# Attention, layer norm and FP4 feed-forward on one core: maxima transposed in 32 by 32 blocks on VectorE and split on GpSimd, loads of stacks and weights in other chunks, another order in the first chunk

## What is computed

```
q, k, v = (x w.T) * s + b          # 16 heads of 16, each weight 256x256
attn    = softmax(q k.T / sqrt(16))
x1      = layernorm(x + (attn v) w_o.T * s_o + b_o)
fq(t)   = blockwise FP4 quantise and dequantise, blocks of 16
h       = silu(fq(x1) fq(w_gate).T) * (fq(x1) fq(w_up).T)      # 704 wide
out     = layernorm(x1 + fq(h) fq(w_down).T)
```

## Time and profile before

| | |
|---|---|
| median of 3 runs | 2092.97 us (2092.76 to 2098.21) |
| profiled execution | 2092.96 us, span 2091.1 us |
| granted TensorE clock, mean | 0.993 |
| PE busy | 2026.4 us, 97% of the span |
| PEld busy | 1055.3 us, 50% |
| DVE busy | 1898.9 us, 91% |
| ACT busy | 1669.0 us, 80% |
| POOL busy | 799.2 us, 38% |
| chain that ended last | PE 83%, DVE 10%, ACT 4%, DMA 1% |
| stages, from the span's start | project to about 210 us, attend to about 1500 us, feed to 2091 us |

### The profile page before, as it was taken

How to read it: one execution, slowest core, us unless ns; L and a number is a source line. 1 busy time by engine, 2 the same in 40 slices (tenths; PEclk the granted TensorE clock), 3 DMA queues, 4 the chain that set the end, 5 groups by cost and what they waited for, 6 DMA issues and landing times.

```text
span 2091.1 us, 42075 instructions
## 1 busy us (share of the span) xinstructions
PE 2026.4 (97%) x15836; PEld 1055.3 (50%) x15836; DVE 1898.9 (91%) x2497; ACT 1669.0 (80%) x3246; POOL 799.2 (38%) x712
## 2 busy tenths in 40 slices
PE   8899999999999999999999999999889999999998
PEld 7677333333333333333333333333477777777776
DVE  4687999999999999999999999998299999999996
ACT  6566888888888888888888888888767777777775
POOL 3000599999100000000000000000168888888885
PEclk9999999999999999999999999999999999999999
DMA  7965632342243234224223322420212222222110
GB/s 211 270 226 214 113 55 49 54 68 48 43 70 57 43 58 64 48 44 76 51 43 63 59 48 48 74 48 13 89 42 61 59 61 61 61 61 61 61 31 21
DMA packets 106615, 153.09 MB, mean 73 GB/s; under 512 B 22124, under 2 KB 68972, under 8 KB 106412
## 3 DMA queue, kind: packets, MB, share of 16 engines
q1 hardware_dynamic: 98732, 142.79, 31.0%
q10 hardware_dynamic: 7392, 7.34, 1.1%
q0 software_dynamic: 288, 0.27, 0.1%
HBM read 89.53 MB, written 59.24 MB: 71 GB/s over the span
## 4 chain that ended last, share of the span: by engine, by line
PE 83%; DVE 10%; ACT 4%; DMA 1%; issue 1%; POOL 1%; SPq 0%; POOLq 0%; ACTq 0%; DVEq 0%
PE ps L860 25%; PE ps L915 23%; PE ps L1184 12%; DVE negmax L1024 9%; PE ps L1206 8%; PE ps L480 4%; PE ps L490 3%; PE ps L1173 3%; PE ps L1195 2%; ACT craw L983 2%; PE ps L1214 1%; DMA qk_parts<-parts 1%; PE ps L884 1%; ACT room L975 1%; PE ps L467 1%
## 5 line engine op out<-in xcount | busy, mean ns | idle before, releaser
L1024 DVE TENSOR_REDUCE negmax<-ps 128x1 f32<-128x1024 f32 x984 | 1189.1, 1221 | 28.6 <-PE ps L860 22.9
L975 ACT ACTIVATE room<-ps 128x512 f32<-128x512 f32 x2048 | 1102.6, 609 | 139.5 <-PE ps L884 109.9
L884 PE MATMUL ps<-qs,ks 50*128 50x512 f32 x2048 | 744.8, 448 | 0.7 <-ACT room L975 0.5
L860 PE MATMUL ps<-ks,qs 48*128 48x512 f32 x1968 | 717.6, 444 | 16.3 <-DVE negmax L1024 16.3
L915 PE MATMUL ps<-room,vals 128*17 128x256 f32 x8192 | 638.0, 385 | 11.3 <-ACT craw L983 1.5
L860 PEld LDWEIGHTS ps<-ks,qs 48*128 48x128 f32 x1968 | 289.8, 184 | 425.3 <-DVE negmax L1024 317.6
L1429 POOL TENSOR_TENSOR ctxT<-cin 128x256 f32<-128x256 f32 x64 | 58.6, 916 | 957.6 <-DMA cin<-rden 957.6
L915 PEld LDWEIGHTS ps<-room,vals 128*17 128x17 f32 x8192 | 139.3, 95 | 375.2 <-issue 206.7
L884 PEld LDWEIGHTS ps<-qs,ks 50*128 50x128 f32 x2048 | 303.7, 184 | 16.9 <-ACT room L975 12.4
L1184 PE MATMUL ps<-wguT,xqT 128*128 128x512 f32 (+1 forms) x1152 | 265.1, 384 | 2.1 <-DVE xqT L1357 2.1
L1184 PEld LDWEIGHTS ps<-wguT,xqT 128*128 128x128 f32 x1152 | 209.3, 189 | 58.6 <-issue 20.2
(11 more groups left out here) (109 smaller groups left out, 2171.4 us busy)
## 6 DMA issues: line engine op xcount, KB each, us to landing
qk_parts<-parts SPq DMA_DIRECT2D x64, 512.0 KB, 3.5
qs<-qk_parts SPq DMA_DIRECT2D x192, 128.0 KB, 4.6
ks<-qk_parts SPq DMA_DIRECT2D x192, 128.0 KB, 7.4
ctx_raw<-craw SPq DMA_DIRECT2D x64, 256.0 KB
cin<-ctx_raw SPq DMA_DIRECT2D x64, 128.0 KB
cin<-rden SPq DMA_DIRECT2D x64, 128.0 KB
xin<-in_L_attn_x_dram SPq DMA_DIRECT2D x32, 256.0 KB, 4.7
out_dram<-fin SPq DMA_DIRECT2D x64, 128.0 KB, 1.7
```

The lines of the kernel that those rows point to most:

```text
L860: return nc.tensor.matmul(ps[:, MX + 2 * (item[i.k, u] % 2) + bank, :], qs[rows, i.slot(RING), pair, t * P:(t + 1) * P], ks[rows, i.slot(R ...
L884: nc.tensor.matmul(ps[:, score_bank(i, s * GH + n), :], ks[rows, slot, pair, kt * P:(kt + 1) * P], qs[rows, slot, pair, qh * BANK:(qh + 1) ...
L975: nc.scalar.activation(prob[:, prob_slot(i, s), score_order(i)[n], :], ps[:, score_bank(i, s * GH + n), :], ACT.Exp, scale=float(D) ** -0. ...
L1024: nc.vector.tensor_reduce(negmax[:, j.slot(RING), max_column(u):max_column(u) + 1], ps[:, bank:bank + 2, :], AX.XY, ALU.max, negate=True). ...
```

## The change

The transpose of the maxima leaves TensorE. VectorE turns `negmax` in blocks of 32 by 32 (`turn`, into `turned_rows`, 128x32), GpSimd makes the high part and the remainder (`part`), and SyncE moves them with eight DMAs of 4 KB each, in pieces of 128 bytes. The turn takes no place in the alternation of the banks (`items` has units alone).

`AHEAD` goes from 4 to 6: the maxima of the next group are done and turned at step 10 instead of 12, and twelve units of group 1 instead of eight run in `project`, four in each of chunks 12 to 14.

GpSimd calls `part` once before the weight quantisation (group 1), once after every eight operations of it, and for the remaining groups after it. It waits each time until that group's maxima are turned.

In `project` the query stack of group 0 is loaded in chunk 2 and the key stack in chunk 3 (both in chunk 2 before), those of group 1 in chunks 8 and 9 (both in 5 before). The first two weights for the scales are loaded in chunks 5 and 7 instead of 0 and 2, so that VectorE makes those scales at the end of chunks 6 and 8. The FFN weights are loaded behind the stack of group 2 instead of ahead of it. Within a block of queries and keys the product with the remainder of x is last. In the first chunk the transposes of w_k and w_v stand before query block 0, with their copies.

```diff
-AHEAD = 4
+AHEAD = 6
 LEAD = 2 * AHEAD
-ARRIVED = 64
+BQ = 32
+ARRIVED = 16 * 2 * (P // BQ)
 PRODUCTS = ((0, 0), (0, 1), (1, 0))
+PROJECTED = ((0, 0), (1, 0), (0, 1))
...
-    def transpose(self, nc, bank, negmax, ident, i):
-        nc.tensor.transpose(bank[0:MU, 0:P], negmax[:, i.slot(RING)], ident[:, :]).then_inc(self.psum, 1)
-
-    def split(self, nc, dve, bank, i, done):
-        dve.wait_ge(self.psum, i.lin(1, 1))
-        wait(dve, self.arrived, i.lin(ARRIVED))
-        nc.vector.tensor_copy(self.mrow[:, 0], bank[0:MU, 0:P]).then_inc(self.chain, 1)
-        dve.wait_ge(self.chain, i.lin(1, 1))
-        nc.vector.tensor_tensor(self.mrow[:, 1], bank[0:MU, 0:P], self.mrow[:, 0].bitcast(F32),
-                                ALU.subtract).then_inc(done, 1)
...
+    def turn(self, nc, dve, negmax, i):
+        wait(dve, self.parted, i.lin(2))
+        nc.vector.transpose(self.turned_rows[:, :], negmax[:, i.slot(RING)]).then_inc(self.turned, 1)
+
+    def part(self, nc, pool, i):
+        pool.wait_ge(self.turned, i.lin(1, 1))
+        wait(pool, self.arrived, i.lin(ARRIVED))
+        nc.gpsimd.tensor_copy(self.mrow[:, 0], self.turned_rows[:, :]).then_inc(self.parted, 1)
+        pool.wait_ge(self.parted, i.lin(2, 1))
+        nc.gpsimd.tensor_tensor(self.mrow[:, 1], self.turned_rows[:, :], self.mrow[:, 0].bitcast(F32),
+                                ALU.subtract).then_inc(self.parted, 1)
+
+    def into_stack(self, sp, qs, i):
+        sp.wait_ge(self.parted, i.lin(2, 2))
+        for part in range(2):
+            rows = qs[KR + part:P:HALF, i.slot(RING)].bitcast(F32).rearrange("a j (t b q) -> a (j t) b q", b=P // BQ,
+                                                                             q=BQ)
+            for b in range(P // BQ):
+                sp.dma_start(rows[:, :, b, :], self.mrow[b * BQ:(b + 1) * BQ, part].bitcast(F32)
+                             ).then_inc(self.arrived, 16)
...
-        if i.k < TURN:
-            return list(range(first, first + MAX_PER))
-
-        return [u if MU <= u < MU + LEAD else None for u in range(first - 1, first - 1 + MAX_PER)]
+        return [u if u < MU + LEAD else None for u in range(first, first + MAX_PER)]
...
-        return {0: 0, 2: 1, NCH - 3: 2}.get(i.k)
+        return {MAX_FROM + 1: 0, MAX_FROM + 3: 1, NCH - 3: 2}.get(i.k)
...
-            group = {MAX_FROM - 2: 0, MAX_FROM + 1: 1}.get(i.k)
-            if group is not None:
-                sp.wait_ge(ones_ready, 2)
-                for n in range(S // C):
-                    sp.wait_ge(qk_stored[n], 64)
-                load_stacks(sp, At(None, group, RING), qk_dram, qs, ks, stack_in)
+            for group, queries in ((0, MAX_FROM - 2), (1, TURN - 4)):
+                if i.k == queries:
+                    for n in range(S // C):
+                        sp.wait_ge(qk_stored[n], 64)
+                    load_stack(sp, At(None, group, RING), 0, qk_dram, qs, stack_in)
+                if i.k == queries + 1:
+                    sp.wait_ge(ones_ready, 2)
+                    load_stack(sp, At(None, group, RING), 1, qk_dram, ks, stack_in)
...
+        weights_by_input(1)
+        weights_by_input(2)
         for i in chunks():
...
             queries_and_keys(i, 0)
-            if i.k == TURN:
-
-                pe.wait_ge(max_whole, 1)
-                maxima_out.transpose(nc, ps[:, MX], negmax, ident, At(None, 0, RING))
             max_unit(i, 0)
             if i.k == 0:
-                weights_by_input(1)
                 queries_and_keys(i, 1)
-                weights_by_input(2)
                 transpose_x(i.plus(1))
...
-                if s == ST - AHEAD and i.ok(NGR - 1):
-                    transpose_max(i.plus(1))
...
                     if s == ST - AHEAD and u == 0 and i.ok(NGR - 1):
-                        bank = MX + 2 * (item[i.k + 1, None] % 2)
-                        maxima_out.split(nc, dve, ps[:, bank], i.plus(1), max_read)
+
+                        dve.wait_ge(max_read, item[i.k + 1, MU - 1] + 1)
+                        maxima_out.turn(nc, dve, negmax, i.plus(1))
...
+            if n[0] % FQ_PER_GROUP == 0:
+                next_maxima()
+
+        def next_maxima():
+            maxima_out.part(nc, pool, At(None, group[0], RING))
+            group[0] += 1
+
+        next_maxima()
         projections_done(pool)
```

More of the change, by code:

```diff
@@ L160, in into_stack, with __init__ @@
-    def into_stack(self, sp, qs, i, done, count):
-        sp.wait_ge(done, count)
-        for half in range(2):
-            rows = slice(half * MU // 2, (half + 1) * MU // 2)
-            for part in range(2):
-                at = half * HALF + KR + part
-                sp.dma_start(qs[at:at + 1, i.slot(RING)].bitcast(F32).rearrange("a j (t q) -> a (j t) q", q=P),
-                             self.mrow[rows, part].bitcast(F32)).then_inc(self.arrived, 16)
+    def __init__(self, turned_rows, mrow, turned, parted, arrived):
+        self.turned_rows, self.mrow, self.turned, self.parted, self.arrived = turned_rows, mrow, turned, parted, arrived
@@ L428, in gpsimd @@
         nc.gpsimd.memset(vals[:, LAST:, :, D:DV], 1.0).then_inc(v_ones, 1)
+        maxima_out.part(nc, pool, At(None, 0, RING))
     def tensor(pe):
@@ L645, in vector @@
         split_x(At(None, 0, 2))
+        split_weights(1)
         for i in chunks():
             if i.k == TURN:
-                maxima_out.split(nc, dve, ps[:, MX], At(None, 0, RING), first_maxima)
+                dve.wait_ge(max_whole, 1)
+                maxima_out.turn(nc, dve, negmax, At(None, 0, RING))
             take_max(i, 0)
@@ L719, in load_x, with load_stack @@
                  ).then_inc(x_in[n], 16)
-def load_stacks(eng, i, qk_dram, qs, ks, stack_in):
-    n = i.slot(RING)
-    for side, stack, order in ((0, qs, PARTS_Q), (1, ks, PARTS_K)):
-        groups = qk_dram[side].rearrange("t b (g j a d) n -> t (b g) a d j n", d=D, a=2, j=GP)
-        for j, part in enumerate(order):
-            for half in range(2):
-                src = groups[part, bass.ds(i.lin(1), 1), half].rearrange("x d j n -> (x d) j n")
-                at = half * HALF + j * D
-                eng.dma_start(stack[at:at + D, n].bitcast(F32), src).then_inc(stack_in[n], 16)
+def load_stack(eng, i, side, qk_dram, stack, stack_in):
+    n = i.slot(RING)
+    groups = qk_dram[side].rearrange("t b (g j a d) n -> t (b g) a d j n", d=D, a=2, j=GP)
+    for j, part in enumerate((PARTS_Q, PARTS_K)[side]):
+        for half in range(2):
+            src = groups[part, bass.ds(i.lin(1), 1), half].rearrange("x d j n -> (x d) j n")
+            at = half * HALF + j * D
+            eng.dma_start(stack[at:at + D, n].bitcast(F32), src).then_inc(stack_in[n], 16)
+def load_stacks(eng, i, qk_dram, qs, ks, stack_in):
+    for side, stack in enumerate((qs, ks)):
+        load_stack(eng, i, side, qk_dram, stack, stack_in)
 def attend(nc, sb, sem, room, qk_dram, vals, ctx_dram, rden_dram, ps, ident, ffn_ws, amax_w, rcp_w,
-           scales_done, ffn_w_in, wguT, wdT, qs, ks, stack_in, negmax, maxima_out, qk_stored, first_maxima, qk_float, v_ready, wt_ready, wt_split, craw, sums,
+           scales_done, ffn_w_in, wguT, wdT, qs, ks, stack_in, negmax, maxima_out, qk_stored, qk_float, v_ready, wt_ready, wt_split, craw, sums,
            craw_stored, rden_ready, rden_stored, x_tok, cin, xin, c_in, x_in):
@@ L1040, in gpsimd @@
         n = [0]
+        group = [1]
         def link(ins):
@@ L1071, in gpsimd @@
         assert n[0] == FQ_STEPS
+        while group[0] < NGR:
+            next_maxima()
     return Programs(sync, gpsimd, tensor, scalar, vector)
```

46 lines of the change are left out of this document (17 added, 29 removed).

## The result

The kernel after takes 2069.68 us, the median of five executions (2068.45 to 2073.56), beside 2092.76 us for the kernel before in the same comparison: a ratio of 0.9888 with a 95% interval of 0.9871 to 0.9905. The forecast was 2069.8. The profiled execution took 2068.45 us with a span of 2066.6, so its span is 24.5 us shorter than before, where the sum of the prediction had 23.1.

A forecast was written before the change was run, and what follows sets the result against it. TensorE's own sequence was taken to bound attention, and TensorE the projection too. Terms: -24.9 + 0 + 2.4 + 2.6 - 1.9 - 1.3 = -23.1 us; 2092.96 - 23.1 = 2069.8 us, range 2060 to 2079.

The forecast's parts named there:

- What bounds attention: Attention: TensorE's sequence sets the pace; taking 30 maxima transposes off it saves 0.83 us each, 24.9 us.
- The turn and the chain: Attention: turn 0.2 us on VectorE; 9.3 us from step 10's TensorE pair to last DMA landing, cover 12.2; cost 0.
- Units: Four maximum units moved from attention to projection: gain 0 in attention, +0.5 and +1.9 us in projection, sum +2.4.
- Scales: Projection chunks 7 and 9: scales delay the first reduction, TensorE's second unit waits about 1.3 us; +2.6 us (0 to +4).
- Chunk 4: Projection: store stall goes, keys 5.5 us late, lower clock 2.5 us; 20.4 for 22.34 us, -1.9 (-8 to +3).
- First chunk: Projection start: w_v delays the first projection 1.1 us, values begin near 17.1 instead of 18.41; -1.3 us (-2.5 to +0.5).
- FFN weights: Loaded behind group 2's stack, ahead of group 1's maxima, which have about 5 us to spare; 0.
- Maxima late: Attention: each group's first score waits, paid 31 times; 2128 us if the eight DMAs follow at 1.3 us; chance 0.05.
- VectorE sets the rate: Attention: VectorE sets the pace, so each group saves only 0.53 us; total 2074 us; chance 0.12.
- Keys in time: Chunk 4: stores and stack loads share the DMA engines, chunk takes 12.4 to 14.4 us; total 2062; chance 0.12.
- keys later still: Chunk 4: keys near 66 us, two stretches at the lower clock, chunk takes 25 us; total 2075; chance 0.12.
- The gap stays: Attention: something else holds TensorE's pair behind the turn; 2095 us with the projection's costs; chance 0.04.

The follow-up runs named there:

- run with the bank turn: Kernel after, but from group 2 on a group's second maximum unit takes the same PSUM bank pair as its first; 2093.55 us, ratio to before 0.9995.

## Why the prediction was right, point by point

*What bounds attention.* Right. The sum had 30 x 0.83 = 24.9, and the stage gave 24.8. It has 31 transposes and not 30, but the one in group 30 has no maximum behind it and gave 0.22. The 29 in groups 1 to 29 gave 0.82 each (23.8), the one in group 0 0.8. The run with the bank turn shows the cause.

*The turn and the chain.* The turn was put at 0.2 and took 0.20. The two operations on GpSimd took 0.21 and 0.26, at or below the lower bound of 0.26. The chain was put at 9.3 us and measures 8.3: the first issue comes 2.8 us after the pair and not 3.1, the eight are 0.54 us apart and not 0.62, and the last lands 1.7 us after it was issued and not 1.9. The cover of 12.2 us was right, and the run with `AHEAD` = 4 shows that the earlier step is needed: at 7.3 us of cover the same chain eats the gain.

The rule of the Trainium skill's page "DMA: Bandwidth & Descriptors" (Specifications), that pieces under 512 B leave line rate, had no effect to be seen here: the eight DMAs of 128-byte pieces were issued closer together (0.54 us) than the four of 512-byte pieces of twice the size (0.62), and the last had landed 1.7 us after its issue, for 1.9. At what rate the pieces themselves moved no run here shows.

*Units.* Right to 0.1: +0.5 in chunk 12 and +1.9 in the last two.

*Scales.* The mechanism was right, two chunks of 13.5 us, and the size 2.2 for 2.6. TensorE's second unit of chunk 7, where the earlier trace rows has no wait:

```profile
101.05 0.50 PE L468 MATMUL ps<-ks,qs 48*128 48x512 f32 x2 [1.01 <-DVE halfmax L588]
```

*Chunk 4.* The mechanism was right: one wait for the keys, none for stores. The keys were 4.1 us late, where I had taken 5.5 from a band of 4 to 6.8. The clock's part was put at 2.5 and is 19.09 - 12.40 - 4.13 = 2.56. The first line is from this execution, the second from the second one of the same kernel:

```profile
57.39 0.79 PE L468 MATMUL ps<-ks,qs 48*128 48x512 f32 x2 [4.13 <-DMA ks<-qk_parts]
```

```profile
59.35 0.80 PE L468 MATMUL ps<-ks,qs 48*128 48x512 f32 x2 [5.16 <-DMA ks<-qk_parts]
```

There chunk 4 took 20.25 us, beside the 20.4 of the forecast. So the miss of 1.4 us is within what single executions of this kernel differ by, and it does not tell that a transfer was priced too long.

One reason given carried less than it seemed. The stall on stores does go since the stores are ahead of the keys (it is back, 5.8 us, when they are not), but that alone gains nothing, as the run with keys and queries together shows: the split merely exchanges the waits, and the removed stage load brings the time. The sum gave that load no term of its own.

*First chunk.* The order's gain was put at 1.3 and is 1.5 to 2.4. At the late clock of the run with the bank turn the replay comes out as written: the first projection starts 1.2 us late (11.26 for 10.04), since it waits for w_v, and the values begin at 17.06, put at 17.1. In the first profile of the kernel after w_v was in time, the first projection starts at 10.20 and the values at 14.59. The other 1.6 to 2.5 us of the profiled -4.0 are the clock's earlier rise in that execution, and no part of the sum spoke of it.

*FFN weights.* 0, as forecast: TensorE has no wait on a DMA in the first two groups of attention.

*What the sum lacked.* A stretch at the lower clock in group 0, +4.4 us, and -1.4 in feed, whose code is untouched; the cause of the latter is open. The misses of start and chunk 4 (-2.7 and -1.4) and these two nearly cancel, so that the median lies 0.1 us from the forecast is luck. Term by term the forecast was good to 1 us in the steady state, and it missed by 1.4 to 4.4 us where the clock moved.

*The rivals.* Maxima late: refuted for `AHEAD` = 6, and its arithmetic (lateness paid in full in each group) confirmed at `AHEAD` = 4. VectorE sets the rate: refuted by the period and by the run with the bank turn; its 0.53 us saved would have been 39.95 a group. Keys in time, keys later still: neither, at 19.09 and 20.25. The gap stays: refuted.

## What to carry to other kernels

When two engines are both busy 97% of a loop, the share does not say which of them holds the other; look for the one place where the pace breaks, and count it. Here an operation of 0.28 us cost 0.82 because it took a place in a two-deep rotation of buffers (and 0.22 where nothing behind it needed them), and a longer chain on three other engines was cheaper once it was started two steps earlier. And when a load is moved out of the way of a stall, ask which consumer needs its data first: moving the consumer by one chunk, with the scale loads put back, brought 7 us by the medians and 3.5 by the two profiled executions, while the other two orders of the loads tried gave nothing (2068.54 and 2069.11 us, one execution each).

## What the runs showed of the chip that was not expected

- A block transpose of 128x32 float32 on VectorE takes 0.20 us, and two more that follow it take 0.26 together.
- A DMA from SBUF to SBUF of 32 pieces of 128 B takes SyncE 0.54 us to issue.
- TensorE's first matmuls take the time of its lower level (eight transposes 1.97 us for 1.03), though the granted clock reads 1.00 there, and when they get short differs from execution to execution, 11.4 to 15.8 us with the new order in the first chunk. Chunk 1 started between 20.9 and 23.7 us in the nine profiles with it, and between 24.6 and 25.4 in the five with the old order.
- The start of attention lost 1.5 to 7 us to a stretch at the lower clock in the eleven profiles of changed kernels and nothing in the three of the kernel before, and work put into its idle places did not keep the clock up.
